# A fourth buffer of normalised rows, five slots, and transposes first in the unit of a mixture-of-experts kernel

## The reference, cut to what matters

```python
x = x + gnn(layernorm(x), adj, Wq, bq, Wk, bk, Wv, bv, Wo, bo)
grouped = layernorm(x).reshape(B, S // t, t, D)                  # t = 16
logits = einsum('bgtd,des->bgtes', grouped, controller) + tie
perm = (logits == max(logits, axis=-3, keepdims=True))           # one token per group and expert
inner = relu(einsum('bgtesf,bgtes->bgesf', einsum('bgtd,desf->bgtesf', grouped, f1), perm))
x = x + einsum('bgesd,bgtes->bgtd', einsum('bgesf,esfd->bgesd', inner, f2), perm)
```

## Time and profile before

| | us |
|---|---|
| median of 3 runs | 862.83 |
| lowest, highest | 857.71, 863.29 |
| the profiled execution | 860.81 |
| its span, first to last instruction | 859.0 |
| attention | 0 to 546.8 |
| first transposes and logits | 546.8 to 559.8 |
| unit stage, expert stage of chunk 0 | 559.8 to 597.9, to 620.8 |
| of chunk 1 | to 664.7, to 687.6 |
| of chunk 2 | to 731.3, to 754.2 |
| of chunk 3 | to 799.0, to about 821 |
| return of the last chunk | to 859.0 |

### The profile page before, as it was taken

One profiled execution on the slowest core, in us unless ns is written; L12 is line 12 of the kernel. 1 busy time (PEld: TensorE's weight loads), 2 busy tenths in 40 slices (PEclk: granted clock), 3 DMA queues, 4 the chain that ended last, 5 costly groups with the idle time before them and its releaser, 6 DMA issues.

```text
span 859.0 us, 22433 instructions
## 1 busy us (share of the span) xinstructions
PE 750.5 (87%) x7252; PEld 573.1 (67%) x7252; DVE 615.0 (72%) x2551; ACT 570.6 (66%) x1654; POOL 119.9 (14%) x116
## 2 busy tenths in 40 slices
PE   5799999999999999999999997477978977977934
PEld 3678788888888888888888885345554544543511
DVE  3598898899899899899889887354545645635512
ACT  2498899998989989999999886143533533532410
POOL 0101001000010010100100100545033124220000
PEclk9899999999999999999999999698989989978967
DMA  5576576675776766757756568000977878779689
GB/s 147 117 172 155 124 171 146 139 173 128 157 161 140 157 143 158 158 128 173 154 130 149 124 142 255 1 2 2 387 243 253 341 264 276 311 243 321 261 310 326
DMA packets 102197, 157.60 MB, mean 183 GB/s; under 512 B 12288, under 2 KB 65024, under 8 KB 101888
## 3 DMA queue, kind: packets, MB, share of 16 engines
q1 hardware_dynamic: 99968, 155.56, 66.0%
q10 hardware_dynamic: 2176, 1.31, 0.6%
HBM read 47.78 MB, written 41.94 MB: 104 GB/s over the span
## 4 chain that ended last, share of the span: by engine, by line
PE 70%; DVE 7%; DMA 6%; POOL 5%; issue 5%; SPq 4%; ACT 2%; ACTq 0%; POOLq 0%; DVEq 0%
PE bank L473 12%; PE bank L425 12%; PE bank L487 7%; PE bank L460 6%; PE bank L447 6%; PE bank L510 6%; POOL h L386 5%; PE bank L642 4%; PE bank L621 3%; PE bank L610 3%; SPq L292 3%; PE bank L573 3%; DMA XRlast<-scratch 2%; PE bank L586 2%; PE bank L418 2%
## 5 line engine op out<-in xcount | busy, mean ns | idle before, releaser
L789 ACT ACTIVATE Ps<-Ps,nmax 128x256 f32<-128x256 f32 x512 | 255.2, 503 | 24.5 <-DVE nmax L984 22.4
L984 DVE CUSTOM_DVE_ANT_0 Ps<-bank,masks 128x256 f32<-128x256 f32 x512 | 198.8, 421 | 24.7 <-issue 22.8
L473 PE MATMUL bank<-ident,Ps 128*128 128x128 f32 x1024 | 146.5, 276 | 1.9 <-ACT Ps L789 1.5
L473 PEld LDWEIGHTS bank<-ident,Ps 128*128 128x128 f32 x1024 | 116.4, 141 | 20.4 <-issue 12.8
L425 PE MATMUL bank<-hT,WT 128*128 128x256 f32 x512 | 125.6, 390 | 0.8 <-ACT hT L746 0.8
L460 PE MATMUL bank<-stack 128*128 128x256 f32 x512 | 117.3, 331 | 6.9 <-DMA stack<-parts 6.7
L425 PEld LDWEIGHTS bank<-hT,WT 128*128 128x128 f32 x512 | 95.6, 196 | 12.4 <-issue 1.1
L374 POOL TENSOR_TENSOR X<-X,bob 128x512 f32 (+1 forms) x32 | 40.8, 1277 | 446.6 <-ACT hn L754 419.8
L386 POOL TENSOR_SCALAR h<-X,mv,root 128x256 f32<-128x256 f32 x60 | 74.8, 1258 | 199.7 <-PE bank L610 143.2
L789 ACT ACTIVATION_READ_ACCUMULATOR Ps<-Ps,nmax 128x1 f32 x512 | 97.9, 191 | 0.0
L995 DVE COPY PTs<-bank 128x512 f32<-128x512 f32 x128 | 87.8, 686 | 5.3 <-PE bank L473 5.2
(11 more groups left out here) (80 smaller groups left out, 1066.4 us busy)
## 6 DMA issues: line engine op xcount, KB each, us to landing
stack<-parts SPq DMA_DIRECT2D x512, 128.0 KB, 2.4
scratch<-stage SPq DMA_DIRECT2D x64, 512.0 KB, 4.1
stage<-scratch SPq DMA_DIRECT2D x48, 512.0 KB, 6.5
X<-in_x SPq DMA_DIRECT2D x32, 256.0 KB, 2.8
out<-X SPq DMA_DIRECT2D x32, 256.0 KB, 5.7
XRlast<-scratch SPq DMA_DIRECT2D x4, 2048.0 KB, 16.4
f1s<-in_L_ffn_f SPq DMA_DIRECT2D x1, 2048.0 KB, 7.6
f2s<-in_L_ffn_f SPq DMA_DIRECT2D x1, 2048.0 KB, 13.0
```

The costliest lines, as they stand in the source:

```text
L473: last = nc.tensor.transpose(PTb[h % 2][:, k * N + t * P:k * N + t * P + P], Ps[:, pr % 2, t, h % 2, k * P:k * P + P], ident[:, :])
L789: last = nc.scalar.activation(Ps[:, pr % 2, t, h, :], Ps[:, pr % 2, t, h, :], ACT.Exp, bias=nmax[:, pr % 2, t, h:h + 1], scale=-1.0, accum ...
L984: last = nc.vector.tensor_tensor_reduce(out=Ps[:, pr % 2, t, h, :], in0=s_bank(n)[:, h * N:h * N + N], in1=masks[:, t, :], scale=1.0, scal ...
```

## The change

`h2` gets four buffers (`NORMS`) instead of three, so that `norm_unit(n)` waits for unit n-4. `stage` gets five slots instead of six, in the expert stages and for the gathers. `h2T` and `h2` lie before `permT`, which is now outside the attention's memory and is zeroed once at the start. The names `NORMS` and `group_maximum` are new. TensorE's order in each unit is: unit transposes of n+2, select 0, one-hot transposes of n+1, scatter, select 1, logits, select 2, scatter, select 3, scatter, as many scatters as the unit has. ScalarE saves `h2T` first. VectorE takes the tied logits before it copies select 2, the maximum after the second `finish` and before it copies select 3.

```diff
--- before.py
+++ after.py
@@ -41,7 +41,8 @@
     CG = CT * GPT
     CP = CG // 2
     QUADS = ES // 4
-    SLOTS = 6
+    SLOTS = 5
+    NORMS = 4
     REGIONS = 7
     AHEAD = 2
     INNERS = 8
@@ -130,16 +131,16 @@
         at[0] = floor
         XS = place("XS", [P, KT, ES, CG])
         stage = place("stage", [P, SLOTS, 4, D])
+        h2T = place("h2T", [P, KT, UT * P])
+        inner = h2T[:, :, :].rearrange("p k (b g) -> p (k b) g", g=CG)
+        h2 = place("h2", [P, NORMS, UT, D])
+        assert at[0] >= attention_end
         permT = place("permT", [P, REGIONS, UT * P])
         permR = place("permR", [P, 2, UT * P])
-        h2T = place("h2T", [P, KT, UT * P])
-        inner = h2T[:, :, :].rearrange("p k (b g) -> p (k b) g", g=CG)
-        h2 = place("h2", [P, 3, UT, D])
         LT = place("LT", [P, UT * P // 2])
         XRlast = nc.alloc_sbuf_tensor_at("XRlast", [P, CT, 4, D], F32, offset=floor)
         XR = stage
         assert max(at[0], attention_end) <= nc.sbuf_usable_end
-        assert attention_end <= floor + 4 * (KT * ES * CG + SLOTS * 4 * D + (REGIONS - AHEAD) * UT * P)
 
         banks = ctx.enter_context(nc.psum_tensor("bank", [P, 8, 512], F32))
         bank = [banks[:, i, :] for i in range(8)]
@@ -360,7 +361,7 @@
             pool.wait_ge(consts, 1)
             nc.gpsimd.affine_select(out=ident[:, :], in_=ident[:, :], compare_op=ALU.not_equal, fill=1.0, base=0,
                                     pattern=[[-1, P]], channel_multiplier=1).then_inc(consts, 1)
-            nc.gpsimd.memset(permT[:, REGIONS - AHEAD:REGIONS, :], 0.0).then_inc(zeroed, 1)
+            nc.gpsimd.memset(permT[:, :, :], 0.0).then_inc(zeroed, 1)
             values = np.linspace(0.0, 1e-6, T).astype(np.float32)
             for t in range(T):
                 nc.gpsimd.memset(tie[:, 0, t:t + 1], float(values[t])).then_inc(zeroed, 1)
@@ -379,15 +380,14 @@
 
             def norm_unit(n):
 
-                if n >= 3:
-                    pool.wait_ge(sel_ready, (n - 2) * UT)
+                if n >= NORMS:
+                    pool.wait_ge(sel_ready, (n - NORMS + 1) * UT)
                 for t in range(UT):
                     tile = n * UT + t
-                    last = nc.gpsimd.tensor_scalar(h2[:, n % 3, t, :], xtile(tile), mv2[:, tile, 0:1],
+                    last = nc.gpsimd.tensor_scalar(h2[:, n % NORMS, t, :], xtile(tile), mv2[:, tile, 0:1],
                                                    root[:, 1, tile:tile + 1], ALU.subtract, ALU.mult)
                 last.then_inc(h2_done, 1)
             norm_unit(1)
-            nc.gpsimd.memset(permT[:, 0:REGIONS - AHEAD, :], 0.0).then_inc(zeroed, 1)
             for n in range(2, CHUNKS * UNITS):
                 norm_unit(n)
 
@@ -571,7 +571,7 @@
                 for k in range(KT):
                     for t in range(UT):
                         last = nc.tensor.transpose(bank[k][:, t * P:t * P + P],
-                                                   h2[:, n % 3, t, k * P:k * P + P], ident[:, :])
+                                                   h2[:, n % NORMS, t, k * P:k * P + P], ident[:, :])
                 last.then_inc(h2T_ready, 1)
 
             def logits(n):
@@ -607,7 +607,7 @@
                 for k in range(KT):
                     for j in range(4):
                         r = slice(32 * j, 32 * j + 32)
-                        last = nc.tensor.matmul(bank[4 + j][:, k * P:k * P + P], h2[r, n % 3, t, k * P:k * P + P],
+                        last = nc.tensor.matmul(bank[4 + j][:, k * P:k * P + P], h2[r, n % NORMS, t, k * P:k * P + P],
                                                 permR[r, n % 2, t * P:t * P + P], start=True, stop=True)
                 last.then_inc(sel_ready, 1)
 
@@ -676,32 +676,22 @@
                 n = c * UNITS + u
                 ahead = n + AHEAD < CHUNKS * UNITS
                 pairs = scatters(u) if c > 0 else ()
-                if len(pairs) == 2:
-                    scatter(c - 1, pairs[0])
+                if ahead:
+                    unit_transpose(n + AHEAD)
                 select(n, 0)
                 if n + 1 < CHUNKS * UNITS:
                     one_hot_transpose(n + 1)
-                if len(pairs) == 3:
-                    if ahead:
-                        unit_transpose(n + AHEAD)
+                if pairs:
                     scatter(c - 1, pairs[0])
-                    select(n, 1)
-                    if ahead:
-                        logits(n + AHEAD)
-                    select(n, 2)
+                select(n, 1)
+                if ahead:
+                    logits(n + AHEAD)
+                select(n, 2)
+                if pairs:
                     scatter(c - 1, pairs[1])
-                    select(n, 3)
+                select(n, 3)
+                if len(pairs) > 2:
                     scatter(c - 1, pairs[2])
-                else:
-                    select(n, 1)
-                    if ahead:
-                        unit_transpose(n + AHEAD)
-                    if len(pairs) == 2:
-                        scatter(c - 1, pairs[1])
-                    select(n, 2)
-                    if ahead:
-                        logits(n + AHEAD)
-                    select(n, 3)
 
             def experts(c):
                 pe.wait_ge(sel_dve, (c + 1) * CT)
@@ -858,16 +848,13 @@
 
             def unit(c, u):
                 n = c * UNITS + u
-                three = c > 0 and len(scatters(u)) == 3
                 ahead = n + AHEAD < CHUNKS * UNITS
+                if ahead:
+                    save_h2T(n + AHEAD)
                 save_selected(c, u, 0)
                 if n + 1 < CHUNKS * UNITS:
                     save_one_hot(n + 1)
-                if three and ahead:
-                    save_h2T(n + AHEAD)
                 save_selected(c, u, 1)
-                if not three and ahead:
-                    save_h2T(n + AHEAD)
                 save_selected(c, u, 2)
                 save_selected(c, u, 3)
 
@@ -1124,15 +1111,18 @@
             def tied_logits(n):
 
                 dve.wait_ge(log_ready, n + 1)
-                link(nc.vector.tensor_tensor(LT[:, :].rearrange("p (g t) -> p g t", t=T),
+                mark(nc.vector.tensor_tensor(LT[:, :].rearrange("p (g t) -> p g t", t=T),
                                              bank[2][:, 0:UT * P // 2].rearrange("p (g t) -> p g t", t=T),
                                              tie[:, :, :].broadcast_to([P, UT * GPT // 2, T]), ALU.add))
-                link(nc.vector.tensor_reduce(gmax[:, :], LT[:, :].rearrange("p (g t) -> p g t", t=T), AX.X, ALU.max))
+
+            def group_maximum():
+
+                chain_wait()
+                mark(nc.vector.tensor_reduce(gmax[:, :], LT[:, :].rearrange("p (g t) -> p g t", t=T), AX.X, ALU.max))
 
             def one_hot(n):
 
-                if n == AHEAD:
-                    dve.wait_ge(zeroed, 2 + T)
+                chain_wait()
                 if n >= REGIONS:
                     dve.wait_ge(sc_ready, (n - REGIONS + 1) * (CT // 2) // UNITS)
                 for half in range(2):
@@ -1158,27 +1148,21 @@
                 n = c * UNITS + u
                 ahead = n + AHEAD < CHUNKS * UNITS
                 pairs = scatters(u) if c > 0 else ()
-                three = len(pairs) == 3
                 save_selected(c, u, 0)
                 if pairs:
                     finish(c - 1, pairs[0])
                 save_selected(c, u, 1)
-                if three:
-                    if ahead:
-                        tied_logits(n + AHEAD)
-                    save_selected(c, u, 2)
-                else:
-                    if pairs:
-                        finish(c - 1, pairs[1])
-                    save_selected(c, u, 2)
-                    if ahead:
-                        tied_logits(n + AHEAD)
-                if three:
+                if ahead:
+                    tied_logits(n + AHEAD)
+                save_selected(c, u, 2)
+                if pairs:
                     finish(c - 1, pairs[1])
+                if ahead:
+                    group_maximum()
                 save_selected(c, u, 3)
                 if ahead:
                     one_hot(n + AHEAD)
-                if three:
+                if len(pairs) > 2:
                     finish(c - 1, pairs[2])
 
             def experts(c):
```

## The result

The changed kernel takes 833.51 us (median of 4 runs, 832.69 to 835.67) against 861.86 us of the kernel before on the same chips: ratio 0.9683, 95% interval 0.9643 to 0.9722. The forecast was 840.0, its range 831 to 854. The profiled execution took 835.67 us, its span is 833.8; 25.2 us less than the span before.

| stretch | before | after | gain |
|---|---|---|---|
| to the first transposes of the expert part | 546.87 | 545.50 | 1.4 |
| from there to the first expand of chunk 0 | 51.03 | 41.67 | 9.4 |
| first expand of chunk 0 to first expand of chunk 3 | 201.12 | 185.38 | 15.7 |
| from there to the end | 59.98 | 61.25 | -1.3 |

A forecast was written before the change was run, and what follows sets the result against it. Chunk 0 was taken as held by GpSimd's normalisation, chunks 1 to 3 by GpSimd and DMA in turn. Gains of 9.7 and 11.2 us (15.7 - 4.5) off the profiled 860.8 gave 840 us, range 831 to 854.

The forecast's parts named there:

- The wait for GpSimd: Unit stages: TensorE's transposes wait 19.4 us in 8 pieces for GpSimd's normalisation; a fourth buffer removes all of it.
- Chunk 0: First unit stage, transposes first with four buffers: units of 6.76 us, 28.4 us against 38.13, gain 9.7.
- Chunks 1 to 3 paced by DMA: Later unit stages: data for three scatters need 11.8 us, TensorE's work 8.5, so DMA sets the pace; gain 15.7.
- Last landing 32.3 us after the start of gathering: Unit stages 1 to 3: sixth gather lands at 12.6 us, remaining gathers and stores take 19.7 more at 332 GB/s.
- The loss by the clock, 4.5 us: Chunks 1 to 3: half clock after TensorE's pauses costs 1.5 us a chunk; bounds nothing and 19.8.
- The pause of 2.2 us before the second scatter of three: Units of chunks 1 to 3: TensorE pauses some 2.2 us there, long enough that half clock may follow, costing 2.2 us.
- A wait is also followed by half clock: TensorE in unit stages: after a wait the same transposes take 1.94 us instead of 1.09, a scatter 1.93 against 1.07.
- The second rival: Chunks 1 to 3: pauses for data bring half clock each time and nothing absorbs it; 855 us, chance 0.2.
- the sum before the deduction: Chunks 1 to 3: gains of 4.9, 4.4 and 6.4 us from DMA pacing, 15.7 in all.
- Five slots at cost 0: Expert and unit stages: a ring of five instead of six costs nothing; 6.5 us left for moves landing within 4.8.
- An expert stage longer than 23 us: Sign named in advance: expert stages above 23 us would disprove the zero cost taken for the slots.
- The order, "nothing more": VectorE and ScalarE: h2T copies ahead of select 0 cost 0.3 us a unit in chunk 0, hidden in the others.

The follow-up runs named there:

- half gathers: Kernel after with each gather fetching two of its four expert rows a partition, so half of the products are left out: 814.6 us, ratio 0.947.

## Why the prediction was right, and where it was off

- **The wait for GpSimd goes, the fourth buffer is the reason.** Right. 19.4 us of waiting were gone, and with three buffers and the new order there are 46.6. It is also true without the order: the buffer alone is worth 22 us.
- **Chunk 0.** 28.4 us were worked out, 28.47 measured from the first of its transposes (558.70) to its expert stage. The mechanism held step by step: select 1, the logits, select 2 and select 3 start within 0.06 us of where they were put.
- **Chunks 1 to 3 paced by DMA.** Right: half gathers end it. Last landing 32.3 us after the start of gathering was the forecast; in chunk 1 the last gather was issued at 640.83 and landed 6.3 us later, 31.8 after 615.36, and in the other two it was 31.0 and 30.6. The rate was a little better than the 332 GB/s that was taken (343 and 353 in the windows shown).
- **The loss by the clock, 4.5 us.** This is the term that was mis-sized. From the first gather to the first expand 35.0 us were worked out before the deduction; 34.2, 33.4 and 35.3 were measured, so no loss of 1.5 us a stage shows in them. The granted clock was 1.00 in stages 1 and 2. Stage 3, with the least work on TensorE, fell to 0.87, and there from scatter 7 to the first expand 3.9 us went by where stage 1 took 3.0. The pause of 2.2 us before the second scatter of three, on which the deduction rested, came as two in stage 1, 0.86 us before it and 0.79 within it, and no wait for a gather was longer than 1.5 us. The sentence "A wait is also followed by half clock" was too general: the earlier trace rows show it, but the same wait at 572.33 us (above) left the clock up. The second rival, half clock at every pause, would have given 855 us and did not come.
- **That chunks 1 to 3 gained 15.7 us, the sum before the deduction, is partly luck.** It is 17.8 us gained from the first gathers on, less 2.1 us ahead of them: 1.2 by the half clock in which the expert stage of chunk 0 began, and 0.9 in which no single step was found. These two losses were not in the sum, and the 17.8 is 2.1 more than the sum had. By chunk 4.9, 4.4 and 6.4 us were forecast; from the first gathers on it was 5.7, 6.0 and 6.2.
- **Five slots at cost 0.** Not wrong for the kernel after as a sum, since its DMA share shows no gap (1.04, 1.07), but the reason given was incomplete. An expert stage longer than 23 us was named as the sign against it, and chunk 0 has one of 23.29. It is not the slots: no staging copy waits for a move in the trace, the granted clock is 0.66 at its start, and the same kernel took 22.07 us there in its second execution. The same edit costs 9 us where scatters are late, and one slot fewer costs 8.9 us in the kernel after (842.4 against 833.5, on different chips). Six slots with four buffers could not be tried: the kernel after leaves 792 bytes of a partition's memory free, and a slot takes 4,096. What a sixth slot would bring stays open.
- **The order, "nothing more".** The text counted its largest effect without naming it: only 2.7 us behind the last landing, since scatter 7 stands just before select 3. That place is worth 6 us. All of the order is worth 14 with four buffers.
- The median gained 28.4 us and the profiled pair 25.2, against 20.9. The difference to the pair is 4.3: 4.5 more in chunks 1 to 3 (15.7 against 11.2, see above), 1.4 at the start, -1.3 at the end and -0.3 in chunk 0 with its lead-in. The start and the end differ as much from run to run.

## What to carry to other kernels

An order that asks for a result first pays only when the producer has been given a buffer early enough to run a whole unit ahead; the same order with one buffer fewer was a loss of 3% against the kernel before, and of 1.5% against the old order with as few buffers and slots. When a ring is fed by its own consumer, its depth is worth what the consumer's delays are: work out the slack for the latest consumer, not for the usual one. Where a stage ends on a transfer, look at what stands behind its last landing and at what shares the queue with it: moving the stores out from between the gathers gave another 1%. And a term taken from one wait with half clock behind it should be checked against the other waits in the same trace before it enters a sum.

## What the runs showed of the hardware

With gathers and stores in flight without a gap, the 16 DMA engines moved 343 to 353 GB/s at a share of 1.04 to 1.07, and a select (0.73 us) and a copy of 128 x 512 (0.69 us on VectorE) took as long beside it as in chunk 0; a normalisation took 4.89 us in chunk 0 and 4.89 or 5.08 beside the gathers. An expert stage that began at half clock took 23.3 us and one that began at full clock 22.07: the same kernel had either in its chunk 0 in different executions (granted clock 0.66 in 587 to 592 us in the profile after). A wait of 1.38 us was followed by half clock in one place and one of 2.73 us was not in another, so the length of a wait alone does not tell what the clock does.
